# Four-layer gated decoder on one core: keys and values of attention layers 3 and 4 projected ahead of their loops

## The chip, the cores and the metric

The kernel runs on one core of one Trainium2 chip. The metric is the device time of one execution in microseconds (us). The kernel uses all engines of the core: PE (TensorE), DVE (VectorE), ACT (ScalarE), POOL (GpSimd) and SP, which issues transfers.

## The reference

A decoder with four stages. Each adds a gated cross-attention and a gated feed-forward network (FFN) to `x` of 64 sequences x 64 tokens x 128 features. `ctx` has the same shape and doesn't change. The sizes written in the helper functions of the reference are not those of the inputs: attention has 16 heads of 8 features and 64 keys per sequence.

```python
x = x + tanh(g_xattn[0]) * L0_attention(q=norm(x), k=ctx, v=ctx)
x = x + tanh(g_ffn[0])   * L0_ffn(norm(x))                      # int8 SwiGLU
x = x + tanh(g_xattn[1]) * L1_attention(k=ctx, q=norm(x), v=ctx, mask)   # causal
x = x + tanh(g_ffn[1])   * L1_moe(norm(x))                      # 8 experts, top 2
x = x + tanh(g_xattn[2]) * L2_attention(q=norm(x), k=ctx, v=ctx)
x = x + tanh(g_ffn[2])   * L2_ffn(norm(x))                      # block-quantised
x = x + tanh(g_xattn[3]) * L3_attention(query=norm(x), key=ctx, value=ctx)
x = x + tanh(g_ffn[3])   * L3_ffn(norm(x))                      # 4-bit quantised
```

Each attention projects queries from the normalised `x`, and keys and values from `ctx` by weights of its own; then come scores, softmax over the 64 keys, the weighted values and an output projection. Keys and values of every layer hang on `ctx` alone.

## The kernel before

Every engine has a program of its own, written out by hand, and they meet at semaphores. The order of the work is the order of the lines; no scheduler moves anything. The 4096 tokens are 32 tiles of 128 (two sequences each), in `x_sb` all through; `ctxT` holds the context turned, features on partitions. Two buffers (s or x = 0, 1) alternate between tiles.

**An attention layer** (`attention(l)`, l = 0 to 3, once on each engine) is a software pipeline. `attention_order` calls `half` for t = -3 to T + 2, with the tiles that each step works on: `new` = t for scores, `ahead` = t + 1 for its key and query, `later` = t + 2 for its normalised rows, `prev` = t - 1, `old` = t - 2 and `oldest` = t - 3 for what comes behind the softmax. In layers 1 and 3 the steps with t < 0 are done elsewhere. In one step PE does, in this order: the scores of tile t (L674, 16 small matmuls); the transposes of `xn` (L640) and of `o_sb` (L649); the key of tile t + 1 (L653) and its query (L655); the values of tile t (L692); the outputs of tile t - 1 (L706, 32 small matmuls); the output projection of t - 2 (L720), in layer 2 with a bias by L722; and the eight transposes of `sm` (L747), the softmax's argument, which end in `ps`. ACT takes the exponential (L1038), copies `oT` and `xnT` out of PSUM (L1052, L1054), writes the values into `vbd` (L975, a block-diagonal operand), the query into `qbd` (L938) and the key into `kT`, twice with different scales (L940; the trace calls the two buffers `q_r` and `q_m`). DVE takes the row maximum (`rowmax`, L1879), subtracts it (`sm`, L1885, two halves), inverts the softmax's denominator (L1825), adds the residual (L1547) and scales the output (L1836). POOL normalises rows (`xn`, L1320). The key of one tile passes like this:

```python
# PE, key_and_query, L651 on
nc.tensor.matmul(project[:, 0:P], wk[l][:, :], ctxT[:, (t + 1) * P:(t + 2) * P], start=True, stop=True)
# ACT, key_and_query, L936 on
last = nc.scalar.activation(kT[y][:, a, :], src[:, 0:P], ACT.Identity, scale=odd_pair[:, a:a + 1], bias=bkp[l][:, a:a + 1])
```

**Layer 2** does more in the same loop: for each tile POOL issues two indirect transfers that gather the experts' rows (L1202), and DVE mixes them into `x_sb` (L1579), until the tiles run out some six steps before the end.

**The routing drain** lies between layer 1 and the experts. Steps T + 3 to T + 9 turn (L543), score (L555) and count (L566 to L571) the last routed tiles. POOL scatters rows to the experts' slots (L1218). When the last tile is chosen, ACT takes the exponential of the gates (L1100); DVE then adds to every tile of `x_sb` the rows that no expert took (L1937, 32 steps), and increments what the experts wait for (L1993). PE runs 26 matmuls whose result nobody reads (`keep_clock`, L509), and then the experts (L768 on).

**The barrier** lies behind the experts. The gathers wait until every expert's output is stored. PE turns the quantised weights of the last FFNs (L812, 20 transposes; ACT copies them, L1124), runs `keep_clock(8)` and enters layer 2, where steps -2, -1 and 0 have a `keep_clock(5)` each.

Of the kernel before, what the change touches and what calls it, by code (L numbers as in the profile page):

```python
# [14 lines left out]
P = 128  # L15
# [25 lines left out]
FP4_WEIGHT_STEPS, MEASURE_STEPS, ROUND_STEPS = 16, 7, 3  # L41
BATCHES = ((0, 8), (8, 16), (16, 22), (22, 27), (27, 32))
# [9 lines left out]
def flamingo(nc, x_d, ctx_d, mask_d, gx_d, gf_d, attn_d, f0_d, moe_d, f2_d, f3_d, const_d, out_d):  # L52
# [28 lines left out]
    def bias_layer(t, since):  # L81


        l, odd = divmod(t - since - 12, 2)
        return l if not odd and 1 <= l < 4 else None

# [78 lines left out]
    with ExitStack() as stack:  # L165
# [132 lines left out]

        def variances(s, i, n):
            return mv_all[:, :].rearrange("p (i s c) -> p s c i", s=NS, c=2)[:, s, 1, i - n + 1:i + 1]  # L300
# [34 lines left out]
        attn_in, small_in, w0_in, blk_in, mask_in = (sem(n) for n in ("attn_in", "small_in", "w0_in", "blk_in", "mask_in"))  # L335
# [5 lines left out]
        ZERO_SET, VBD_SET, ONES_SET, RSTD_FIRST, RAW_TURNED, WMAX_SHARED = 1, NS + 1, 3 * NS + 1, 3 * NS + 2, 3 * NS + 3, 3 * NS + 4  # L341
# [5 lines left out]
        v_psum, v_taken = sems("v_psum"), sems("v_taken")  # L347
        bst_ready = sems("bst_ready")
# [20 lines left out]
        out_done, scatters_late = sem("out_done"), sem("scatters_late")  # L369
# [5 lines left out]
        def _(sp):  # L375
# [44 lines left out]
            for a in range(2):  # L420
                sp.dma_start(amask_u8[a * S:(a + 1) * S, :].rearrange("q (b k) -> q b k", k=S), mask_d.rearrange("b q k -> q b k")).then_inc(mask_in, 16)
# [62 lines left out]
        def _(pe):  # L484
# [20 lines left out]
            def keep_clock(n, out=bank(1, 2)):  # L505


                for _ in range(n):
                    nc.tensor.matmul(out, ones_b[:, :], amask[:, 0:512], start=True, stop=True, skip_group_check=True)  # L509
# [109 lines left out]
            def attention(l):  # L619
                k = ATTENTION_STAGE[l]  # L620

                def half(t, x, fetch, further, later, ahead, new, prev, old, oldest):
# [64 lines left out]
                    if new is not None:  # L687
                        for b in range(2):
                            for a in range(2):
                                cols = wv[l][:, :].rearrange("d (r a w) -> d a r w", a=2, w=2 * HD)[:, a, :, :]  # L690
                                dst = turned[1][a * S:(a + 1) * S, b * S:(b + 1) * S].rearrange("p (r w) -> p r w", r=RG)
# [1392 lines left out]
```

## Time and profile before

| | |
|---|---|
| three runs, us | 1084.51, 1085.5, 1087.7 (median 1085.5) |
| span of the profiled execution, us | 1084.4 |
| PE busy | 898.7 us, 83% |
| PE weight loads busy | 707.4 us, 65% |
| DVE busy | 885.9 us, 82% |
| ACT busy | 686.2 us, 63% |
| POOL busy | 523.1 us, 48% |

The profiled execution's own time is its span. Busy shares are means over the whole kernel. Where each stage lies, by the trace: layer 1 with the routing ends at about 384 us, the drain lasts to 437, the experts to 531, the barrier to 553, attention 2 to 705, its FFN to 794, attention 3 to 926, and the last FFN to the end. A row of the timeline gives the start, the duration, the engine, the line and the names; in brackets stands how long the engine was idle before it and what ended that. Matmuls of the same line that follow each other are merged in one row. A row of the groups by line gives the names and shapes, the count, the busy time in us, the mean of one in ns, and the idle time in us in front of them with what ended it. A row of a stretch gives its limits and length, busy us (and count) of PE, PE's weight loads, DVE, ACT and POOL, the granted clock of PE as a share of its full 2.4 GHz (0.50 is 1.2 GHz), the share of the DMA engines and GB/s.

### The profile page before, as it was taken

To read this page: it belongs to the slowest core of one execution; us is meant where nothing else is said; L and a number is where in the kernel's file an instruction comes from. 1 tells how busy PE (TensorE), PEld (TensorE's weight loads), DVE (VectorE), ACT (ScalarE), POOL (GpSimd) and SP (SyncE) were. 2 spreads that over 40 slices of the span, in tenths; PEclk is the share of its full clock that TensorE was granted. 3 is DMA by queue.
4 is the path that set the end of the run, shared out by engine and by line. 5 is a ranking of instruction groups with operands and counts; after the bars stand their busy time and mean duration, and the time that the engine had idled before them with its cause. 6 is when DMAs were issued, how large, how long until landed. Compare 5 with 4: busy or idle time off the path is not lost.

```text
span 1084.4 us, 30129 instructions
## 1 busy us (share of the span) xinstructions
PE 898.7 (83%) x11539; PEld 707.4 (65%) x11557; DVE 885.9 (82%) x2296; ACT 686.2 (63%) x1794; POOL 523.1 (48%) x612
## 2 busy tenths in 40 slices
PE   8999999999999932999689999978899999434443
PEld 5888889978887721566457778834478888222222
DVE  6999888878999961567568889889978888899997
ACT  6888864377776610444447777866678888555553
POOL 6444412254367676223287787255553332355554
PEclk9999999999999966899889999988899999655665
DMA  8760000000000012365111111000000000000000
GB/s 214 186 241 2 3 2 2 1 2 3 3 24 27 27 46 76 114 187 175 51 33 32 26 31 29 6 1 2 1 2 2 2 3 3 1 10 16 15 15 24
DMA packets 60526, 44.42 MB, mean 41 GB/s; under 512 B 15196, under 2 KB 55781, under 8 KB 59366
## 3 DMA queue, kind: packets, MB, share of 16 engines
q1 hardware_dynamic: 55718, 34.09, 10.6%
q0 software_dynamic: 4096, 8.34, 2.7%
q8 instruction: 90, 1.47, 0.6%
q14 instruction: 46, 0.38, 0.1%
q10 hardware_dynamic: 576, 0.13, 0.1%
HBM read 23.73 MB, written 18.87 MB: 39 GB/s over the span
## 4 chain that ended last, share of the span: by engine, by line
PE 63%; DVE 21%; issue 6%; POOL 5%; ACT 2%; DVEq 2%; DMA 1%; POOLq 0%; another core or an unknown queue 0%; SPq 0%; ACTq 0%
PE ps L747 10%; PE ps L706 9%; PE ps L674 7%; PE ps L586 4%; PE ps L720 4%; PE ps L692 4%; POOL q_out L1232 3%; DVE rowmax L1879 3%; PE ps L782 3%; PE ps L791 3%; PE ps L783 3%; PE ps L640 2%; PE ps L655 2%; PE ps L653 2%; DVE sm L1885 2%
## 5 line engine op out<-in xcount | busy, mean ns | idle before, releaser
L1879 DVE TENSOR_REDUCE rowmax<-ps 128x16 f32<-128x1024 f32 x128 | 155.8, 1217 | 35.7 <-PE ps L674 34.4
L1885 DVE TENSOR_TENSOR sm<-ps,rowmax 128x512 f32<-128x512 f32 x256 | 164.9, 686 | 3.4
L1038 ACT ACTIVATE pr<-ps 128x512 f32<-128x512 f32 x256 | 138.9, 595 | 38.2 <-PE ps L747 36.0
L747 PE MATMUL ps<-cst,sm 128*128 128x128 f32 x1024 | 138.9, 277 | 13.3 <-DVE sm L1885 12.2
L706 PE MATMUL ps<-vbd,pr 128*64 128x18 f32 x4096 | 140.3, 211 | 0.5 <-ACT pr L1038 0.5
L706 PEld LDWEIGHTS ps<-vbd,pr 128*64 128x64 f32 x4096 | 134.2, 138 | 1.4 <-ACT pr L1038 1.3
L1320 POOL TENSOR_SCALAR xn<-x_sb,mv_all,rstd_all 128x128 f32<-128x128 f32 x122 | 98.2, 805 | 71.7 <-PE ps L640 65.7
L747 PEld LDWEIGHTS ps<-cst,sm 128*128 128x128 f32 x1024 | 112.8, 141 | 26.3 <-issue 19.5
L938 ACT ACTIVATE qbd<-ps,bqp,cst 128x128 f32<-128x128 f32 x256 | 104.6, 463 | 6.2 <-PE ps L655 2.4
L975 ACT ACTIVATE vbd<-ps 64x128 f32<-64x128 f32 x256 | 70.8, 277 | 34.2 <-PE ps L692 26.6
L1202 POOL DMA_INDIRECT big<-expert_out,row_g x64 | 68.2, 1066 | 49.9 <-DMA expert_out<-xn_all 22.8
L1218 POOL DMA_INDIRECT slots<-xn_all,row_s x64 | 65.0, 1015 | 35.8 <-DVE sm L1885 16.9
L1232 POOL TENSOR_TENSOR big<-big 128x640 f32<-128x640 f32 (+2 forms) x36 | 39.0, 1105 | 82.8 <-DVE big L1761 62.8
L606 PE MATMUL ps<-ident_b,q_out 128*128 128x128 bf16 x64 | 11.5, 277 | 78.8 <-POOL q_out L1232 78.6
L1194 POOL TENSOR_TENSOR rstd_all<-mv_all,cst 128x1 f32<-128x1 f32 x64 | 36.1, 567 | 78.2 <-DVE mv_all L1864 37.8
L1052 ACT ACTIVATE oT<-ps 128x128 f32<-128x128 f32 x128 | 35.5, 277 | 49.1 <-PE ps L649 47.3
L606 PEld LDWEIGHTS ps<-ident_b,q_out 128*128 128x128 bf16 x64 | 4.2, 106 | 92.6 <-POOL q_out L1232 89.0
L1208 POOL TENSOR_TENSOR rstd_all<-mv_all,cst 128x1 f32<-128x1 f32 x60 | 34.5, 575 | 61.3 <-DVE mv_all L1858 50.3
L720 PE MATMUL ps<-wo,oT 128*128 128x128 f32 x256 | 61.0, 320 | 1.2 <-ACT oT L1052 1.2
L1232 POOL TENSOR_TENSOR q_out<-q_r,q_s 128x1280 bf16<-128x1280 f32 (+2 forms) x18 | 37.9, 2104 | 47.7 <-DVE q_r L1692 45.1
L1547 DVE SCALAR_TENSOR_TENSOR x_sb<-ps,tg,x_sb 128x128 f32<-128x128 f32 x192 | 55.0, 290 | 5.2 <-PE ps L857 2.9
L692 PE MATMUL ps<-wv,ctxT 128*64 128x64 f32 x1024 | 58.1, 235 | 0.1
(299 smaller groups left out, 2348.3 us busy)
## 6 DMA issues: line engine op xcount, KB each, us to landing
slots<-hT SPq DMA_DIRECT2D x8, 1024.0 KB, 11.0
sm<-slots SPq DMA_DIRECT2D x32, 256.0 KB, 3.3
expert_out<-xn_all SPq DMA_DIRECT2D x16, 256.0 KB, 3.0
ew<-in_L_ffn_w SPq DMA_DIRECT2D x24, 128.0 KB, 2.6
out<-x_sb SPq DMA_DIRECT2D x32, 64.0 KB, 1.5
slots<-xn_all,row_s POOLq DMA_INDIRECT x64
big<-expert_out,row_g POOLq DMA_INDIRECT x64
x_sb<-in_x SPq DMA_DIRECT2D x1, 512.0 KB, 4.6
```

The costliest lines, as they stand in the source:

```text
L674: last = nc.tensor.matmul(bank(0, r)[:, b * P:(b + 1) * P], qbd[x][rows, b * S:(b + 1) * S, :].rearrange("d q h -> d (q h)"), kT[x][rows, ...
L692: last = nc.tensor.matmul(dst, ctxT[:, t * P + b * S:t * P + (b + 1) * S], cols, start=True, stop=True, skip_group_check=True)
L706: last = nc.tensor.matmul(dst[:, :, h2, :], probs[:, h2, :], heads[:, :, h2, :], start=True, stop=True, skip_group_check=True)
L720: last = nc.tensor.matmul(mixed[:, M_Y], oT[x][:, :], wo[l][:, :], start=True, stop=(l != 2))
L747: last = nc.tensor.transpose(turned[b][:, r * P:(r + 1) * P], sm[x][:, c:c + P], ident)
L938: nc.scalar.activation(qbd[y][:, :, a], src[:, P:2 * P], ACT.Identity, scale=parity[:, a:a + 1], bias=bqp[l][:, a:a + 1])
L975: last = nc.scalar.activation(dst, src[part, :].rearrange("p (r h w) -> p r h w", h=2, w=HD), ACT.Copy)
L1038: nc.scalar.activation(pr[y][:, b, :], turned[b], ACT.Exp, scale=SCALE).then_inc(p_ready[y], 1)
L1232: return nc.gpsimd.tensor_tensor(dst.rearrange("p (n w) -> p n w", w=width), src.rearrange("p (n w) -> p n w", w=width), factor.unsqueeze( ...
L1320: nc.gpsimd.tensor_scalar(xn[buf][:, :], xt, mv_all[:, 2 * u:2 * u + 1], rstd_all[:, u:u + 1], ALU.subtract, ALU.mult).then_inc(xn_ready[b ...
L1879: v.tensor_reduce(row3, sc, AX.X, ALU.max).then_inc(rowmax_ready[x], 1)
L1885: v.tensor_tensor(sm[x][:, :].rearrange("p (r g k) -> p r g k", r=RG, k=S)[:, part], sc[:, part], row3[:, part].unsqueeze(3).broadcast_to( ...
```

## The change

The keys and values of layers 2 and 3 (`KEPT`) are no longer projected inside the layers' loops. They are projected in groups of four tiles: a key group is one matmul with 512 columns, a value group 16 matmuls with 64, each into a PSUM bank of its own out of four (two groups in flight). ACT copies each group to SBUF unscaled, 16 copies per layer, into buffers that are idle there (`big`, `gate`, `ew`, `amask`, `xn_all`) and one new one (`v_late`). In the loops ACT builds `kT` and `vbd` from SBUF. Layer 2's eight groups are projected in the routing drain. Of layer 3's, five come after the weight transposes in the barrier, and three in steps -3, -2 and -1 of layer 2. PE waits for all copies of layer 2 before the experts, and for all of layer 3 at t = 0 of layer 2. `keep_clock(8)` in the barrier and `keep_clock(5)` in steps -2 and -1 of layer 2 go; the idle matmuls now read `cst`, since `amask` is overwritten. The filling of `vbd` waits for the outputs of two tiles before (`o_psum`), not for values in PSUM. Two semaphores are merged into others, which changes no order. The diff, cut:

```diff
+GROUP, GROUPS, KEPT = 4, T // 4, (2, 3)
...
+    def kept_number(l, g):
+        return GROUPS * (l - 2) + (g if l == 2 else (g - GROUPS // 2) % GROUPS)
...
+        kept_keys = {
+            2: [big[:, c:c + GW] for c in (1024, 1536, 2048, 2560, 7168, 7680)] + gate,
+            3: [big[:, 3328 + g * GW:3328 + (g + 1) * GW] for g in range(GROUPS - 1)] + [ew[0][:, 0:2, :].rearrange("p n d -> p (n d)")]}
+        kept_values = {
+            2: [a[:, g * GW:(g + 1) * GW] for a in (amask[:, :].bitcast(F32), v_late) for g in range(GROUPS // 2)],
+            3: [xn_all[:, g * GW:(g + 1) * GW] for g in range(GROUPS)]}
...
+            def value_products(l, t, dst):
+                for b in range(2):
+                    for a in range(2):
+                        cols = wv[l][:, :].rearrange("d (r a w) -> d a r w", a=2, w=2 * HD)[:, a, :, :]
+                        last = nc.tensor.matmul(dst[a * S:(a + 1) * S, b * S:(b + 1) * S].rearrange("p (r w) -> p r w", r=RG),
+                                                ctxT[:, t * P + b * S:t * P + (b + 1) * S], cols, start=True, stop=True, skip_group_check=True)
+                return last
+            def keys_ahead(l, g):
+                n = kept_number(l, g)
+                if n >= 2:
+                    pe.wait_ge(ahead_kept, 2 * n - 3)
+                nc.tensor.matmul(bank(0, 2 * (n % 2)), wk[l][:, :], ctxT[:, g * GW:(g + 1) * GW], start=True, stop=True, skip_group_check=True
+                                 ).then_inc(ahead_psum, 1)
+            def values_ahead(l, g):
+                n = kept_number(l, g)
+                if n >= 2:
+                    pe.wait_ge(ahead_kept, 2 * n - 2)
+                for t in range(GROUP):
+                    last = value_products(l, g * GROUP + t, bank(0, 1 + 2 * (n % 2))[:, t * P:(t + 1) * P])
+                last.then_inc(ahead_psum, 1)
...
                         if ahead is not None:
-                            nc.tensor.matmul(project[:, 0:P], wk[l][:, :], ctxT[:, (t + 1) * P:(t + 2) * P], start=True, stop=True)
+                            if l not in KEPT:
+                                nc.tensor.matmul(project[:, 0:P], wk[l][:, :], ctxT[:, (t + 1) * P:(t + 2) * P], start=True, stop=True)
...
+                    if l == 2 and t == 0:
+                        pe.wait_ge(ahead_kept, 4 * GROUPS)
...
-                    if l == 2 and -2 <= t <= 0 or l == 3 and t == 0:
+                    if l == 2 and t < 0:
+                        keys_ahead(3, t + 4)
+                        values_ahead(3, t + 4)
+                    if l in KEPT and t == 0:
                         keep_clock(5, mixed)
...
             for t in range(T + 3, T + 10):
                 turn_routed(t, 1 - t % NS)
+                if t > T + 3:
+                    keys_ahead(2, t - T - 4)
                 reuse_routing_bank(t, t % NS)
                 score_routed(t, 1 - t % NS)
                 count_batch(t)
+                if t > T + 3:
+                    values_ahead(2, t - T - 4)
+            for g in range(GROUPS - 2, GROUPS):
+                keys_ahead(2, g)
+                values_ahead(2, g)
...
             keep_clock(26)
+            pe.wait_ge(ahead_kept, 2 * GROUPS)
...
+            for g in (4, 5, 6, 7, 0):
+                keys_ahead(3, g)
+                values_ahead(3, g)
             pe.wait_ge(wt_ready, 5)
             pe.wait_ge(early_eps[0], EARLY + 1)
-            keep_clock(8)
...
+            def keep_keys(l, g):
+                n = kept_number(l, g)
+                act.wait_ge(ahead_psum, 2 * n + 1)
+                nc.scalar.activation(kept_keys[l][g], bank(0, 2 * (n % 2)), ACT.Copy).then_inc(ahead_kept, 1)
...
-                    last = nc.scalar.activation(kT[y][:, a, :], src[:, 0:P], ACT.Identity, scale=odd_pair[:, a:a + 1], bias=bkp[l][:, a:a + 1])
+                    last = nc.scalar.activation(kT[y][:, a, :], keys, ACT.Identity, scale=odd_pair[:, a:a + 1], bias=bkp[l][:, a:a + 1])
...
+                    if new is not None and l in KEPT:
+                        act.wait_ge(o_psum[x], IT * l + new)
+                        values(x, tile_of(kept_values[l], t))
...
             for t in range(T + 3, T + 10):
                 empty_routed(t, 1 - t % NS)
+                if t > T + 3:
+                    keep_keys(2, t - T - 4)
+                    keep_values(2, t - T - 4)
+            for g in range(GROUPS - 2, GROUPS):
+                keep_keys(2, g)
+                keep_values(2, g)
             act.wait_ge(e_ready, 1)
             nc.scalar.activation(ge[:, 0, :], ge[:, 1, :], ACT.Exp).then_inc(e_ready, 1)
```

How the instructions stand on PE in the last steps of the drain, before (`xrT` is a routed tile turned, `oh` its choices, `hid` an expert's rows):

```order
L543 MATMUL ps<-cst,xn_all 128x128
L555 MATMUL ps<-rw,xrT 128x8
L566 MATMUL ps<-oh,tri_b 128x80
L568 MATMUL ps<-carry,ones_b 128x80
L571 MATMUL ps<-oh,ones_b 128x2x32
L571 MATMUL ps<-oh,ones_b 128x2x24
L571 MATMUL ps<-oh,ones_b 128x2x16
L571 MATMUL ps<-oh,ones_b 128x2x8
L509 MATMUL ps<-amask,ones_b 128x512 x26
L773 MATMUL ps<-cst,hid 128x128 x8
```

And after the change (L544 is a key group, L536 a value group; the last turn of a routed tile stands in the first row):

```order
L587 MATMUL ps<-cst,xn_all 128x128
L544 MATMUL ps<-ctxT,wk 128x512
L599 MATMUL ps<-rw,xrT 128x8
L536 MATMUL ps<-wv,ctxT 64x64 x16
L544 MATMUL ps<-ctxT,wk 128x512
L536 MATMUL ps<-wv,ctxT 64x64 x16
L544 MATMUL ps<-ctxT,wk 128x512
L610 MATMUL ps<-oh,tri_b 128x80
L612 MATMUL ps<-carry,ones_b 128x80
L615 MATMUL ps<-oh,ones_b 128x2x32
```

Two groups and a key now stand in front of the last count, and five groups and a value group between it and the 26 idle matmuls. On ACT, with their waits, before:

```order
L930 ACTIVATE xrT<-ps 128x128 [waits rT_psum1]
L1100 ACTIVATE ge<-ge 128x32 [waits e_ready]
L934 ACT_TABLE_LOAD
```

and after, the last of the sixteen copies:

```order
L994 ACTIVATE gate_both<-ps 128x512 [waits ahead_psum]
L1003 ACTIVATE v_late<-ps 128x512 [waits ahead_psum]
L1182 ACTIVATE ge<-ge 128x32 [waits e_ready]
L989 ACT_TABLE_LOAD
```

The exponential of the gates stands behind all copies. PE in the barrier, from the weight transposes to the first scores, before:

```order
L812 MATMUL ps<-ident_b,big 128x128 x20
L509 MATMUL ps<-amask,ones_b 128x512 x8
L640 MATMUL ps<-cst,xn 128x128
L509 MATMUL ps<-amask,ones_b 128x512 x5
L653 MATMUL ps<-ctxT,wk 128x128
L655 MATMUL ps<-xnT,wq 128x128
L640 MATMUL ps<-cst,xn 128x128
L509 MATMUL ps<-amask,ones_b 128x512 x5
L674 MATMUL ps<-q_r,qbd 128x128 x8
```

and after, from the last of six groups on:

```order
L544 MATMUL ps<-ctxT,wk 128x512
L536 MATMUL ps<-wv,ctxT 64x64 x16
L684 MATMUL ps<-cst,xn 128x128
L544 MATMUL ps<-ctxT,wk 128x512
L536 MATMUL ps<-wv,ctxT 64x64 x16
L700 MATMUL ps<-xnT,wq 128x128
L684 MATMUL ps<-cst,xn 128x128
L544 MATMUL ps<-ctxT,wk 128x512
L536 MATMUL ps<-wv,ctxT 64x64 x16
L721 MATMUL ps<-q_r,qbd 128x128 x8
```

Six groups stand in front of the first turn of `xn` (L640, now L684), and two more between it and the first scores (L674, now L721).

## Rows read from the trace of the kernel before

**Rows 1.** Groups by line, DVE, mixing part of attention 2 (573.5 to 680.5 us)

```profile
L1825 DVE RECIPROCAL rden<-ps 128x16 f32<-128x16 f32 x22 | 5.7, 258 | 11.5 <-PE ps L722 9.0 <-remote 2.3
```

**Rows 2.** Timeline of one tile of attention 3

```profile
851.48 0.54 PEld L674 LDWEIGHTS ps<-q_r,qbd 32*128 32x128 f32 x16 [0.22 <-ACT q_r L940]
852.27 1.22 DVE L1879 TENSOR_REDUCE rowmax<-ps 128x16 f32<-128x1024 f32 x1 [0.57 <-PE ps L674]
...
852.30 0.30 PEld L653 LDWEIGHTS ps<-ctxT,wk 128*128 128x128 f32 x2
...
852.95 0.31 PEld L692 LDWEIGHTS ps<-wv,ctxT 128*64 128x64 f32 x8
...
853.45 0.56 ACT L975 ACTIVATE vbd<-ps 64x128 f32<-64x128 f32 x2 [0.33 <-PE ps L692]
...
856.39 1.23 DVE L1879 TENSOR_REDUCE rowmax<-ps 128x16 f32<-128x1024 f32 x1 [0.56 <-PE ps L674]
```

**Rows 3.** Timeline, first tiles of attention 3

```profile
798.83 1.22 DVE L1879 TENSOR_REDUCE rowmax<-ps 128x16 f32<-128x1024 f32 x1 [1.44 <-PE ps L674]
...
800.92 1.16 PE L747 MATMUL ps<-cst,sm 128*128 128x128 f32 x8 [0.16 <-DVE sm L1885]
...
802.84 1.23 DVE L1879 TENSOR_REDUCE rowmax<-ps 128x16 f32<-128x1024 f32 x1 [0.97 <-PE ps L674]
```

**Rows 4.** Groups by line and shape, ACT, whole span

```profile
L940 ACT ACTIVATE q_r<-ps,bkp,odd_pair 128x128 f32<-128x128 f32 x128 | 51.4, 459 | 0.0
...
L949 ACT ACTIVATE hT<-x_sb,mean_in,rstd_all 128x128 f32<-128x128 f32 x32 | 14.0, 497 | 0.0
```

**Rows 5.** Timeline of two tiles in the mixing part of attention 2

```profile
579.97 1.00 POOL L1202 DMA_INDIRECT big<-expert_out,row_g  x1 [0.30 <-issue]
...
580.07 0.39 PE L722 MATMUL ps<-y_bias_b,cst 128*128 128x128 f32 x2
...
581.57 0.26 DVE L1825 RECIPROCAL rden<-ps 128x16 f32<-128x16 f32 x1 [0.90 <-PE ps L722]
...
603.89 0.39 PE L722 MATMUL ps<-y_bias_b,cst 128*128 128x128 f32 x2
...
604.31 1.01 POOL L1202 DMA_INDIRECT big<-expert_out,row_g  x1 [0.30 <-issue]
...
605.84 0.26 DVE L1825 RECIPROCAL rden<-ps 128x16 f32<-128x16 f32 x1 [0.79 <-remote]
```

**Rows 6.** Timeline, row maxima of the last tiles of attention 2

```profile
688.93 1.22 DVE L1879 TENSOR_REDUCE rowmax<-ps 128x16 f32<-128x1024 f32 x1 [0.48 <-PE ps L674]
...
701.70 1.23 DVE L1879 TENSOR_REDUCE rowmax<-ps 128x16 f32<-128x1024 f32 x1 [0.51 <-PE ps L674]
```

**Rows 7.** Timeline of the routing drain and the first expert

```profile
399.66 0.23 ACT L1100 ACTIVATE ge<-ge 128x32 f32<-128x32 f32 x1 [6.96 <-issue]
...
402.88 1.38 DVE L1937 SCALAR_TENSOR_TENSOR x_sb<-xn_all,wx,x_sb  x4 [0.18 <-issue]
...
430.25 7.88 DVE L1937 SCALAR_TENSOR_TENSOR x_sb<-xn_all,wx,x_sb  x20 [5.25 <-issue]
...
437.64 2.05 PE L782 MATMUL ps<-q_r,ew 128*128 128x512 f32 x2 [1.65 <-DVEq L1993]
...
443.83 1.02 PE L782 MATMUL ps<-q_r,ew 128*128 128x512 f32 x2
```

**Rows 8.** Busy time and granted clock of two stretches, drain and barrier

```profile
392.00:394.00 2.00, 0.96 (x4) 0.60 (x3) 1.03 (x8) 0.28 (x1) 1.69 (x2) 0.50 0.20 66
540.00:542.00 2.00, 0.93 (x3) 0.51 (x5) 0.96 (x5) 0.00 (x0) 1.55 (x2) 0.50 0.27 66
```

**Rows 9.** Timeline of the barrier behind the experts

```profile
534.01 0.38 PE L812 MATMUL ps<-ident_b,big 128*128 128x128 bf16 x4 [0.29 <-ACT wT L1124]
...
549.55 0.73 PE L674 MATMUL ps<-q_r,qbd 32*128 32x128 f32 x16
...
553.50 1.19 DVE L1879 TENSOR_REDUCE rowmax<-ps 128x16 f32<-128x1024 f32 x1
```

More of the change, by code:

```diff
@@ L85, in bias_layer, with tile_of @@
         return l if not odd and 1 <= l < 4 else None
+    def kept_number(l, g):
+        return GROUPS * (l - 2) + (g if l == 2 else (g - GROUPS // 2) % GROUPS)
+    def tile_of(groups, t):
+        return groups[t // GROUP][:, t % GROUP * P:(t % GROUP + 1) * P]
     def turned_context(t):
@@ L508, in keep_clock @@
                 for _ in range(n):
-                    nc.tensor.matmul(out, ones_b[:, :], amask[:, 0:512], start=True, stop=True, skip_group_check=True)
+                    nc.tensor.matmul(out, ones_b[:, :], cst[:, 0:256].bitcast(BF16), start=True, stop=True, skip_group_check=True)
+            def value_products(l, t, dst):
[18 more added lines that the diff above has]
+                last.then_inc(ahead_psum, 1)
             def turn_context(t):
@@ L686, in half @@
                         pe.wait_ge(p_ready[y], 2 * (IT * l + prev) + 2)
[L687 to L691, printed above, removed]
-                                last = nc.tensor.matmul(dst, ctxT[:, t * P + b * S:t * P + (b + 1) * S], cols, start=True, stop=True, skip_group_check=True)
-                        last.then_inc(v_psum[x], 1)
+                    if new is not None and l not in KEPT:
+                        value_products(l, t, turned[1][:, 0:P]).then_inc(v_psum[x], 1)
                     if oldest is not None:
@@ L847, in ffn2 @@
                     pe.wait_ge(hid_ready[0], IT)
-                    nc.tensor.matmul(bank(0, 1)[:, 0:P], wk[3][:, :], ctxT[:, 0:P], start=True, stop=True)
                 if px is not None:
@@ L934, in load_table, with keep_values, key_and_query @@
                 nc.scalar.activation(g_sb[:, 0:1], tg[:, 0:1], func)
-            def key_and_query(l, y, src):
+            def keep_keys(l, g):
+                n = kept_number(l, g)
+                act.wait_ge(ahead_psum, 2 * n + 1)
+                nc.scalar.activation(kept_keys[l][g], bank(0, 2 * (n % 2)), ACT.Copy).then_inc(ahead_kept, 1)
+            def keep_values(l, g):
+                n = kept_number(l, g)
+                if (l, g) == (3, 0):
+                    for p in range(2):
+                        for s in range(NS):
+                            act.wait_ge(eo_stored[p][s], 16 * E // 2)
+                act.wait_ge(ahead_psum, 2 * n + 2)
+                nc.scalar.activation(kept_values[l][g], bank(0, 1 + 2 * (n % 2)), ACT.Copy).then_inc(ahead_kept, 1)
+            def key_and_query(l, y, src, t):
+                keys = tile_of(kept_keys[l], t) if l in KEPT else src[:, 0:P]
                 for a in range(2):
@@ L1063, in half @@
                         project_ahead()
+                    if l == 2 and t < 0:
+                        keep_keys(3, t + 4)
+                        keep_values(3, t + 4)
                     if l == 0 and t == T:
@@ L1125, in _ @@
             load_table(ACT.Exp)
+            for g in (4, 5, 6, 7, 0):
+                keep_keys(3, g)
+                keep_values(3, g)
+            act.wait_ge(ahead_kept, 2 * GROUPS)
             attention(2)
+            act.wait_ge(ahead_kept, 4 * GROUPS)
             def ffn2(c, x, h, px, ph):
```

30 lines of the change are left out of this document (17 added, 13 removed).

## The prediction

> **What bounds the kernel now.** The change touches four places: the routing drain (about 384 to 437 us), the barrier behind the experts (531 to 553), and the third and fourth attention layers, called attention 2 and attention 3 as in the code (553 to 705 and 794 to 926). I went to each in turn. The first view to read is the list of groups by line, for DVE, in the part of attention 2 where the experts' rows are gathered and mixed in [rows 1]: 22 tiles take 107 us, 4.86 each, and what DVE waited for was the softmax's denominator, 11.5 us in front of the reciprocal. Whether PE or the gathers stand behind that wait decides what the change can give here; it is taken up below.
>
> Attention 3 has no gathers. In order of time [rows 2], rowmax starts at 852.27 and again at 856.39, a period of 4.12 us. Between them PE has 0.30 us of weight loads for the key projection and 0.31 for the values; ACT waits 0.33 for the values before it can fill vbd; and DVE waits 0.57 for scores. Two tiles at the start of the layer show the floor that lies under this [rows 3]: there PE reached the transposes of sm early and waited 0.16 us for DVE, and the rowmaxes still stand 4.01 us apart (798.83 to 802.84), with DVE waiting for scores before each. That loop is rowmax, sm, the last four transposes, the next tile's scores, rowmax; no key or value projection is in it.
>
> **Attention 3.** Removed per tile: one key matmul and four value matmuls, about 0.5 us of PE (0.30 and 0.31 less their overlap with neighbours) [rows 2]. That is not the gain. PE now arrives early, and sm is what it waits for: the period falls from 4.12 to the 4.01 of the floor, which gives 0.11. With some 28 tiles in that state the term is **-3.1 us**. ACT could be late next, since kT and vbd now come from SBUF. The nearest rows are L949, which reads SBUF, at 497 ns, and L940, which reads PSUM, at 459 [rows 4]: 38 ns more on each of four instructions is 0.15, against the 0.33 wait that goes. So ACT gains 0.18 where 0.11 is needed, and stays just off the path. Bounds: 0 (ACT takes over the loop) and -0.5 a tile, -15 (all the removed PE time is gained, which the floor excludes).
>
> **Attention 2.** In the mixing part nothing is gained, by this reading [rows 5]. The reciprocal at 581.57 waited 0.90 us, and the profile names PE's L722, which had ended at 580.46. If that were the cause the lag would be constant. It is 1.11 there, and 1.56 at 605.84, where L722 ended by 604.28. Measured from the end of POOL's gather (580.97, 605.32) the two lags are 0.60 and 0.52. So I hold that POOL releases DVE, not PE. Term 0; bounds -8 (rival A) and +5 (the gathers fall less well between DVE's steps). The last four tiles have no gathers and run like attention 3. Three of their periods take 12.77 us, 688.93 to 701.70 [rows 6], 4.26 each; down to the floor of 4.01 that is 0.25, four times: **-1.0**, between 0 and that.
>
> **The routing drain.** Added to PE from about 392, where its last matmuls on routed tiles stand [rows 8]: eight groups of one 512-column key matmul and sixteen value matmuls. A pair with 512 columns takes 1.02 us at 443.83, at full clock, and 2.05 at 437.64, at half [rows 7]; a tile of values 0.31 [rows 2]. So a group is 1.02 + 4 x 0.31 = 2.3 us, or 4.5 at half. PE is at half clock here, 0.50 over 392 to 394 [rows 8], and the experts' first matmuls took 6.2 us (437.64 to 443.83) to leave it. 6.2 us at half hold 1.4 groups, 6.6 more take 15: PE is done at about 413.5. Three things stand behind it. The batch count waits for two and a half groups; the scatters that need its rows are queued behind others that POOL issues without a pause, so I cost that at nothing (some 10 us of cover). The 26 clock matmuls start later, nothing. But the exponential of the gates, 399.66 now, stands behind all sixteen copies on ACT, so it moves to about 414, and DVE's loop that adds the routed rows (32 steps) with it. Twelve of its 32 steps were done by 430.25; the other 20 then took 7.88 us, and PE's first expert matmul waited 1.65 us for the end of that loop [rows 7]. With 16 us instead of 30 ahead of 430.25, half of the twelve are done, and six more at 0.39 come behind: **+2.4**. Bounds: +4.7 (none of the twelve done) and -1.65 (the loop is done in time). Why the later ones of the twelve were so slow the trace does not say: four of the first six took 1.38 us together, at 402.88, and scatters ran beside those as well [rows 7]. So I take the slowness as something the first half escaped, and the term as it stands. A rule of the Trainium skill reads it otherwise. "GPSIMD Engine Reference", key points, has GpSimd sharing its SBUF interfaces with VectorE, with contention for DVE instructions that have two SBUF inputs, as this one has. By it no step beside the scatters would be quick, so a loop that starts at 414 does hardly any of the twelve, and the term goes to its upper bound, +4.7; the quick steps at 402.88 speak against it.
>
> **The barrier.** PE's last weight transpose ends at 534.39, and tile 0's scores were at 549.55 [rows 9]. Removed are 18 clock matmuls; added, in front of the first transpose of xn, six groups, 13.8 us: to 548. Two more stand in front of the scores, which must also wait for ACT's last copies: 553 plus 1 is 554. The scores themselves can be late, since rowmax started only at 553.50, 3.2 us after their end, behind DVE's mixing; scores at 554 give a rowmax at about 554.8 (0.79 behind them, as at 851.48 and 852.27) [rows 2]: **+1.3**. This takes the full clock, as the dense work behind 437.64 came to it. Bounds: 0, and +12 (six groups at half clock, 27 us).
>
> **Sum.** -3.1 - 1.0 + 2.4 + 1.3 = -0.4 us. The profiled execution spans 1084.4, 0.1% under the median of the three runs, 1085.5; I take the difference off the median: **1085.1 us**.
>
> **Rivals.** *A, PE does pay in attention 2.* The profile names L722 for 9.0 of the 11.5 us in front of the reciprocal [rows 1], and with 0.5 us less work L722 comes 0.5 earlier. If that freed DVE, about 0.3 of each of some 25 tiles would go: -7.5, so 1077.6. Against it are the two lags. Chance 0.20. *B, slower: the block in the barrier runs at half clock.* PE has been thinly busy before it, and the clock was 0.50 over 540 to 542, where the clock matmuls start [rows 8]. If it falls under the added block, six groups take 27 us instead of 14, and the first rowmax comes some 12 us late. The sum is then +10: 1096; half of that, a clock that comes back inside the block, 1090. The change is slower than before once this place costs more than 1.7 us, and measurably so from 5.0. For it: that half clock. Against it: dense work brings the clock back within 6.2 us [rows 7]. Chance 0.17. *C, attention 3 pays nothing*, because ACT's SBUF reads take what its wait gave, and the periods stay: +3.7 (1089) for all of it, or +2.7 (1088) with the tail of attention 2 gained. For it, only 0.07 us a tile separates ACT from the path; against, the wait of 0.33 does go. Chance 0.13. My forecast has 0.50.
>
> **How the numbers follow.** A measurement of this kernel tells a change from none at about 0.3%, 3.3 us: 1082.2 and 1088.8 are the limits. The forecast's own range is 1081 to 1088.5 (the drain from -1.65 to +4.7, the barrier up to +2.5), a fifth of it under 1082.2: faster 0.10, same 0.38, slower 0.02. A gives faster 0.20. B gives slower 0.16, same 0.01. C gives same 0.07, slower 0.06. Together: faster 0.30, same 0.46, slower 0.24. The range of 8 in 10 takes in A, C and the milder half of B: 1077 to 1090.
>
> **What would show it.** Right, if in attention 3 the rowmaxes stand 3.95 to 4.05 apart and PE waits for sm before most transposes; if the mixing part of attention 2 keeps about 4.86 a tile; if the exponential comes at 410 to 416 and the first expert matmul 1 to 4 us later than 437.64; and if the first rowmax of attention 2 comes 1 to 3 us later counted from the experts' end. Wrong, if the period in attention 3 is 4.1 with ACT in front of the scores (C), or under 3.9 (then the floor was misread); if tiles of attention 2 fall under 4.6 (A); or if the clock is half over 534 to 550 (B).

## The result, and the profile after

The changed kernel takes **1104.3 us** (median of 4 runs, 1100.4 to 1108.4), against 1085.5 before: a ratio of **1.017**, interval 1.0149 to 1.0192. It is slower by some 19 us, where I forecast no change, and outside my range (1077 to 1090). Measured again the ratio was 1.0181 (1.0157 to 1.0206). The profiled execution spans 1101.3 us, 16.9 more than the one of before.

Where they come from, by the distance between landmarks that both traces have (us). The first expert matmul is L782 (now L835), the last weight transpose L812 (now L866), rowmax L1879 (now L1966).

| stretch | before | after | difference | forecast |
|---|---|---|---|---|
| start to last rowmax of attention 1 | 377.99 | 378.98 | +1.0 | 0 |
| drain: to the first expert matmul | 59.65 | 79.49 | **+19.8** | +2.4 |
| experts: to the last weight transpose | 96.37 | 96.61 | +0.2 | 0 |
| barrier: to the first rowmax of attention 2 | 19.49 | 23.45 | **+4.0** | +1.3 |
| attention 2, first to last rowmax | 148.20 | 142.74 | **-5.5** | -1.0 |
| to the first rowmax of attention 3 | 93.14 | 94.24 | +1.1 | 0 |
| attention 3, first to last rowmax | 127.34 | 123.58 | **-3.8** | -3.1 |
| to the end | 162.22 | 162.21 | 0.0 | 0 |

The loops gained what they could, and more than I gave them. The drain took it back twice. The list of waits of the changed kernel, over the drain (384 to 460 us; line waited for, us in total, times, longest), says how:

```profile
PEld ps L536 <- issue: 27.4, 28, 2.5
DVE gk L2008 <- ACT ge L1182: 22.0, 1, 22.0
ACT amask L1003 <- remote: 21.6, 2, 18.5
DVE pre L1691 <- PE ps L615: 21.5, 1, 21.5
...
PE ps L536 <- issue: 19.1, 27, 1.7
...
POOL slots L1305 <- DVE row_s L1734: 8.7, 1, 8.7
```

PE stood still 19.1 us inside the value matmuls (L536), and what ended these gaps is "issue": no semaphore, no engine. In the code none of these matmuls but a group's first waits for anything. (The label alone would not show that; in the second experiment it also stands in front of waits for a semaphore.) The timeline of PE shows the shape:

```profile
396.70 1.12 PE L544 MATMUL ps<-ctxT,wk 128*128 128x512 f32 x2
397.76 0.50 PE L536 MATMUL ps<-wv,ctxT 128*64 128x64 f32 x9
398.67 0.26 PE L536 MATMUL ps<-wv,ctxT 128*64 128x64 f32 x1 [0.41 <-issue]
400.08 0.30 PE L536 MATMUL ps<-wv,ctxT 128*64 128x64 f32 x2 [1.15 <-issue]
401.52 0.26 PE L536 MATMUL ps<-wv,ctxT 128*64 128x64 f32 x1 [1.15 <-issue]
...
417.05 0.34 PE L536 MATMUL ps<-wv,ctxT 128*64 128x64 f32 x1 [0.46 <-issue]
417.31 2.08 PE L544 MATMUL ps<-ctxT,wk 128*128 128x512 f32 x2
419.18 0.27 PE L610 MATMUL ps<-oh,tri_b 128*128 128x80 bf16 x1
...
443.48 5.79 PE L530 MATMUL ps<-cst,ones_b 128*128 128x512 bf16 x26
...
458.47 2.05 PE L835 MATMUL ps<-q_r,ew 128*128 128x512 f32 x2 [8.33 <-DVEq L2080]
```

The first group and part of the second run at the pace I took for them. From 398.3 on, one to three matmuls come through every 0.7, 1.4 or 2.1 us. A single one is still short (0.22 to 0.37 us); what is missing is the next one. The last count (L610) stands behind it, at 419.18; it was at 396.33 before, so it comes 22 us later, counted from the end of attention 1. ACT was late as well: its copy of the first value group, whose matmuls had ended at 396.8, started at 414.22, though ACT had been free since 395.7 (timeline, ACT):

```profile
414.22 0.60 ACT L1003 ACTIVATE amask<-ps 128x512 f32<-128x512 f32 x1 [18.48 <-remote]
```

POOL's timeline has the other half:

```profile
413.36 0.97 POOL L1305 DMA_INDIRECT slots<-xn_all,row_s  x1 [0.30 <-issue]
422.98 0.97 POOL L1305 DMA_INDIRECT slots<-xn_all,row_s  x1 [8.65 <-DVE row_s L1734]
...
434.47 0.97 POOL L1305 DMA_INDIRECT slots<-xn_all,row_s  x1 [0.30 <-issue]
```

POOL's scatters ran one behind the other up to 414.3. PE picked up its pace 3 us later. POOL then had nothing to scatter, since the rows of the last tiles hang on the late count; from 422.98 to 435.4 it scattered the rest, and PE stalled again from 427.2 to 437.2. The cover that I gave the count was there, and larger than my 10 us: before, the rows stood ready at 399.5 and the first of these ten scatters was issued at 413.8. But the count came 22 us late, and the last scatter ended 9 us later than before (435.4 against 426.3). What comes behind all copies came last (timeline, ACT and DVE):

```profile
444.08 0.22 ACT L1182 ACTIVATE ge<-ge 128x32 f32<-128x32 f32 x1
...
446.48 0.63 DVE L2024 SCALAR_TENSOR_TENSOR x_sb<-xn_all,wx,x_sb  x2 [0.35 <-DVE wx L2014]
447.29 11.83 DVE L2024 SCALAR_TENSOR_TENSOR x_sb<-xn_all,wx,x_sb  x30 [0.18 <-issue]
```

The exponential moved from 399.66 [rows 7] to 444.08. DVE's 32 steps lie whole between it and the experts; with the scatters over, they take 12.6 us with hardly a gap.

In attention 3 the floor was read right. These rows answer to those of before [rows 2, 3]:

```profile
867.30 1.22 DVE L1966 TENSOR_REDUCE rowmax<-ps 128x16 f32<-128x1024 f32 x1 [0.48 <-PE ps L721]
...
868.03 0.63 ACT L1045 ACTIVATE vbd<-xn_all 64x128 f32<-64x128 f32 x2
...
870.49 0.54 PEld L721 LDWEIGHTS ps<-q_r,qbd 32*128 32x128 f32 x16 [0.17 <-ACT q_r L1010]
871.28 1.23 DVE L1966 TENSOR_REDUCE rowmax<-ps 128x16 f32<-128x1024 f32 x1 [0.48 <-PE ps L721]
```

The period is 3.98 us, and `vbd` waits for nobody. What SBUF costs ACT is in the groups by shape:

```profile
L1010 ACT ACTIVATE q_r<-ps,bkp,odd_pair 128x128 f32<-128x128 f32 x64 | 25.7, 459 | 0.0
...
L1010 ACT ACTIVATE q_r<-big,bkp,odd_pair 128x128 f32<-128x128 f32 x52 | 22.7, 487 | 0.0
...
L1045 ACT ACTIVATE vbd<-xn_all 64x128 f32<-64x128 f32 x64 | 19.8, 309 | 0.4
```

28 ns more for a key copy and 32 for a value copy (277 before): 0.12 us a tile, where I had 0.15.

### The profile page after: what moved, and what is told of

Read it like the earlier page. It is cut to its first block, busy times and chain, and to the rows that moved or that the text cites. A ratio compares the mean times of both kernels' runs of the same rounds, so it can differ in the third digit from the quotient of the medians.

```text
span 1101.3 us, 29957 instructions
## 1 busy us (share of the span) xinstructions
PE 920.1 (84%) x11443; PEld 701.8 (64%) x11443; DVE 882.6 (80%) x2296; ACT 707.4 (64%) x1826; POOL 522.3 (47%) x612
## 4 chain that ended last, share of the span: by engine, by line
PE 65%; DVE 21%; issue 6%; POOL 3%; ACT 2%; DVEq 1%; DMA 0%; SPq 0%; POOLq 0%; another core or an unknown queue 0%; ACTq 0%
PE ps L793 10%; PE ps L748 9%; PE ps L721 6%; PE ps L536 4%; PE ps L630 4%; PE ps L762 4%; DVE rowmax L1966 3%; PE ps L835 3%; POOL q_out L1319 3%; PE ps L844 3%; PE ps L836 3%; PE ps L684 2%; DVE sm L1972 2%; PE ps L700 2%; PE ps L640 2%
## 5 line engine op out<-in xcount | busy, mean ns | idle before, releaser
L1966 DVE TENSOR_REDUCE rowmax<-ps 128x16 f32<-128x1024 f32 x128 | 155.8, 1217 | 35.6 <-PE ps L721 34.2
L793 PE MATMUL ps<-cst,sm 128*128 128x128 f32 x1024 | 143.6, 279 | 23.4 <-DVE sm L1972 20.1
L748 PE MATMUL ps<-vbd,pr 128*64 128x18 f32 x4096 | 143.1, 213 | 0.7 <-ACT pr L1108 0.5
L793 PEld LDWEIGHTS ps<-cst,sm 128*128 128x128 f32 x1024 | 110.3, 141 | 46.5 <-issue 34.7
L536 PE MATMUL ps<-wv,ctxT 128*64 128x64 f32 x1024 | 58.3, 239 | 21.6 <-issue 21.5
L536 PEld LDWEIGHTS ps<-wv,ctxT 128*64 128x64 f32 x1024 | 42.4, 144 | 44.6 <-issue 32.9
```

Source lines behind the costliest of these rows:

```text
L536: last = nc.tensor.matmul(dst[a * S:(a + 1) * S, b * S:(b + 1) * S].rearrange("p (r w) -> p r w", r=RG), ctxT[:, t * P + b * S:t * P + (b ...
L748: last = nc.tensor.matmul(dst[:, :, h2, :], probs[:, h2, :], heads[:, :, h2, :], start=True, stop=True, skip_group_check=True)
L793: last = nc.tensor.transpose(turned[b][:, r * P:(r + 1) * P], sm[x][:, c:c + P], ident)
L1966: v.tensor_reduce(row3, sc, AX.X, ALU.max).then_inc(rowmax_ready[x], 1)
```

## The experiments

**Is it the order on ACT alone?** In this kernel the exponential stands in front of the copies of groups 2 to 7:

```diff
             for t in range(T + 3, T + 10):
                 empty_routed(t, 1 - t % NS)
                 if t > T + 3:
                     keep_keys(2, t - T - 4)
                     keep_values(2, t - T - 4)
+                if t == T + 5:
+                    act.wait_ge(e_ready, 1)
+                    nc.scalar.activation(ge[:, 0, :], ge[:, 1, :], ACT.Exp).then_inc(e_ready, 1)
...
-            act.wait_ge(e_ready, 1)
-            nc.scalar.activation(ge[:, 0, :], ge[:, 1, :], ACT.Exp).then_inc(e_ready, 1)
```

> The changed kernel with one thing moved: on ACT the exponential of the gates stands in front of the copies of groups 2 to 7, not behind all sixteen. Starvation (PE gets its instructions too slowly while POOL's scatters run one behind the other, so the added stretch of small matmuls stalls, and the count behind it comes late): PE's gaps named issue stay (about 19 us in the drain), the exponential comes a few us behind the late count, at about 423 us, PE is through its groups at about 443 as now, and the first expert matmul moves from 458.5 to 446 to 452; in all 1091 to 1098 us. Order on ACT alone (the step of the prediction): the exponential comes at 400 to 404, the first expert matmul at 438 to 441, in all 1084 to 1088.

Measured: 1103.6 us, ratio 1.0155 (1.0126 to 1.0183). PE's gaps are there again (21.2 us named issue), the exponential comes at 421.26 and the first expert matmul at 451.44, 6 us nearer to attention 1 than in the changed kernel. So the place on ACT accounts for 6 of the 20 us, and PE's stall stands with either order: DVE's loop is over at 444.2, and the experts wait for PE itself, which is through its groups at 444.6. The total I expected (1091 to 1098) was missed. The drain's 6 us and 2.9 in the experts were given back, 3.2 in the barrier (26.64 us), 4.5 in attention 2 (147.28) and 2.1 behind it; these lengths differ between kernels with the same loop, as below.

**Is it the number of small instructions?**

```diff
-                for t in range(GROUP):
+                if l == 2:
+                    last = nc.tensor.matmul(bank(0, 1 + 2 * (n % 2)), wv[l][:, :], ctxT[:, g * GW:(g + 1) * GW], ...)
+                for t in range(GROUP if l == 3 else 0):
                     last = value_products(l, g * GROUP + t, bank(0, 1 + 2 * (n % 2))[:, t * P:(t + 1) * P])
```

> The changed kernel in which each value group of layer 2 is one matmul with 512 columns instead of sixteen with 64: about the same PE time (1.0 us against 1.2 at full clock), 4 instructions instead of 64; the values of attention 2 are not the reference's. The order on ACT stays. Starvation by the number of instructions: no gaps named issue over 1 us, PE through the groups by 412 to 418, the exponential at 412 to 418, first expert matmul at 438 to 444, in all 1083 to 1090 us. Contention for SBUF or PSUM, or the half clock, as the cause: the same data stream is read and written, so the groups stay slow, PE ends near 440 and the time stays over 1098.

Measured: 1096.3 us, ratio 1.0092 (1.0062 to 1.0122): a miss for both. Five groups go through without a gap named issue, and the last count is in time, at 398.4. But from 400 on ACT's copies are late, and PE with them (timeline of both engines):

```profile
401.81 1.02 PE L544 MATMUL ps<-ctxT,wk 128*128 128x512 f32 x2
...
404.83 0.60 ACT L996 ACTIVATE big<-ps 128x512 f32<-128x512 f32 x1 [2.24 <-PE ps L552]
...
405.48 1.12 PE L544 MATMUL ps<-ctxT,wk 128*128 128x512 f32 x2 [1.72 <-issue]
409.06 0.60 ACT L1005 ACTIVATE amask<-ps 128x512 f32<-128x512 f32 x1 [3.63 <-remote]
...
409.71 2.07 PE L552 MATMUL ps<-ctxT,wv 128*128 128x512 f32 x2 [3.10 <-issue]
412.62 0.60 ACT L996 ACTIVATE big<-ps 128x512 f32<-128x512 f32 x1 [2.96 <-PE ps L552]
...
413.27 2.07 PE L544 MATMUL ps<-ctxT,wk 128*128 128x512 f32 x2 [1.49 <-issue]
```

ACT copies the groups in their order, keys before values. The copy at 412.62 is that of the fifth key group, whose matmul (401.81) had ended at 402.8, and ACT's copy before it was over at 409.66: ACT itself was 3 us late, and it executes a handful of instructions here. PE was not: a group may start only when the copy of two groups before has emptied its bank, and each of these gaps ends 0.05 us behind such a copy (405.43, 409.66, 413.22), whatever the label says. So on PE the stall went with the sixteen small matmuls. ACT is late without any long stream, and the exponential, behind all copies, came at 432.07.

**Is it the scatters?** Both kernels without 26 of the 28 scatters of the drain (their rows don't reach the experts, which compute with what the buffer held):

```diff
-                    for c in range(2):
+                    for c in range(2 if u == T - 1 else 0):
                         scatter(b, u, c)
...
-            sp.wait_ge(sent, 16 * 2 * T)
+            sp.wait_ge(sent, 16 * 2 * (T - 13))
```

> The changed kernel without 26 of the 28 scatters that POOL issues in the routing drain (tiles 18 to 30; those rows don't reach the experts); the two of tile 31 stay, so the experts still wait for the last choice. If the scatters are what starves the engines: the gaps named issue in the drain are gone, PE's eight groups are through by 412 to 416 (starting at about 392, 1.4 groups at half clock, the rest at full), the exponential comes by 417, DVE's 32 steps take 12.6 us without a gap, first expert matmul at 430 to 433. If the count of small instructions alone does it (an instruction stream that PE cannot be fed at this pace anywhere): the gaps stay with about 19 us, and PE ends near 440.

> The kernel before without the same 26 scatters. If the scatters starve every engine and not PE alone: DVE's loop over 32 tiles, which stood idle for some 24 us between its first 12 steps before, runs through in 12.6 us from 402 on, and ends at 415. If its slowness is its own (its branch, its registers): it keeps steps 2 to 5 us apart and ends near 438.

Measured, the changed kernel: the eight groups run from 392.3 to 411.0, somewhat earlier than I expected, with no gap of PE inside a group,

```profile
396.90 1.15 PE L536 MATMUL ps<-wv,ctxT 128*64 128x64 f32 x32
397.99 1.12 PE L544 MATMUL ps<-ctxT,wk 128*128 128x512 f32 x2
398.95 0.20 PE L610 MATMUL ps<-oh,tri_b 128*128 128x80 bf16 x1
...
409.89 1.15 PE L536 MATMUL ps<-wv,ctxT 128*64 128x64 f32 x32
411.20 5.56 PE L530 MATMUL ps<-cst,ones_b 128*128 128x512 bf16 x25 [0.16 <-issue]
```

the exponential at 411.58, and the first expert matmul at 427.42. The kernel before: DVE's loop over the tiles, with 24.4 us of gaps named issue in the original (one of them is the 5.25 before 430.25 [rows 7]), runs through. Its line in the list of waits of the original, and its rows without scatters:

```profile
DVE x_sb L1937 <- issue: 24.4, 9, 5.2
...
403.98 0.63 DVE L1937 SCALAR_TENSOR_TENSOR x_sb<-xn_all,wx,x_sb  x2 [0.35 <-DVE wx L1927]
404.79 11.37 DVE L1937 SCALAR_TENSOR_TENSOR x_sb<-xn_all,wx,x_sb  x30 [0.18 <-issue]
```

That settles what the gaps hang on. Without the scatters the same instructions run at pace, on PE and ACT in one kernel and on DVE in the other. The edit takes away POOL's issuing and the transfers together, so it doesn't say which of the two it is. (The times of the two, 1083.3 and, from a single run, 1068.6 us, also leave out the scatters' own 26 x 1.28 us, and are no measure of a useful kernel. Nor is the drain: it is 49.32 against 35.97 us, 13.4 apart. With no scatters to wait for, the delay of the exponential (33.5 us behind attention 1 against 21.4) is paid in full. What such a delay costs beside scatters is in the kernels below that keep the keys alone.)

**Which layer, and which part, is worth keeping?** Layer 3 alone, keys and values:

```diff
-GROUP, GROUPS, KEPT = 4, T // 4, (2, 3)
+GROUP, GROUPS, KEPT = 4, T // 4, (3,)
```

(with the drain's calls taken out and the counts adapted)

> Only layer 3 (attention 3) is projected ahead; attention 2 projects in its loop as before, nothing is added to the routing drain, the barrier keeps its five groups and the three in steps -3 to -1. Starvation in the drain as the main loss: the drain is as before (first expert at 437 to 439), attention 3 keeps its 3.98 us a tile (-3.8), the barrier costs up to 4, in all 1083 to 1088 us; attention 2 goes back to about 4.8 a tile. Rival (the loss has its seat in the barrier or in SBUF reads of the loops): over 1095.

Measured: 1091.1 us, ratio 1.0042 (1.0027 to 1.0057). The drain is as before (59.63), attention 3 at 3.98 a tile, attention 2 back at 148.83; but the barrier costs 6.5 us (26.01). The total is 3 us over what I expected, and the barrier is why. Its groups meet POOL's gathers. In the changed kernel PE stands still 2.4 us among the value matmuls there (timeline, PE):

```profile
561.34 0.62 PE L536 MATMUL ps<-wv,ctxT 128*64 128x64 f32 x9
562.37 0.22 PE L536 MATMUL ps<-wv,ctxT 128*64 128x64 f32 x1 [0.41 <-issue]
563.08 0.33 PE L536 MATMUL ps<-wv,ctxT 128*64 128x64 f32 x3 [0.50 <-issue]
564.52 0.81 PE L536 MATMUL ps<-wv,ctxT 128*64 128x64 f32 x19 [1.11 <-issue]
```

With layer 3 alone it is 1.5 us, the granted clock is 0.54 to 0.61 over the first group (533 to 537), and the scores of tile 0 wait 2.8 us for ACT's last copy (list of waits, 533 to 559 us):

```profile
PE ps L721 <- ACT xn_all L995: 2.8, 1, 2.8
...
PE ps L536 <- issue: 1.5, 2, 1.1
```

Then the keys alone, of both layers, with the values in the loops, the idle matmuls restored, and the exponential in front of the copies of groups 2 to 7 as in the first experiment:

```diff
-                    if new is not None and l not in KEPT:
+                    if new is not None:
                         value_products(l, t, turned[1][:, 0:P]).then_inc(v_psum[x], 1)
...
             for g in (4, 5, 6, 7, 0):
                 keys_ahead(3, g)
-                values_ahead(3, g)
```

> Only the keys of both layers are projected ahead (one matmul of 512 columns a group, 4 instructions); the values stay in the loops; the idle matmuls of the barrier are back; the exponential stands in front of the copies of groups 2 to 7. Starvation: the drain is nearly as before (first expert at 437 to 441). Attention 3: the key matmul is about half of the PE time that the change takes away, and 0.14 us a tile is all that the loop can give, so 3.98 to 4.05 a tile; attention 2 between 4.60 and 4.78; in all 1076 to 1083 us. Rival: it takes the values out too to reach the floor (ACT's wait for the values stays), attention 3 stays at 4.08 to 4.12, in all 1083 to 1088.

Measured: **1082.9 us against 1086.7, ratio 0.9968** (0.9952 to 0.9983), faster than before by 0.3%, and within what I expected. Attention 3 is at 3.98 a tile with the value matmuls still in its loop. The drain is 59.90 us, the barrier 19.55, both as before. Two variants of it:

> Only the keys of layer 3 are projected ahead (five groups in the barrier, three in steps -3 to -1 of attention 2, the idle matmuls there kept); nothing in the drain, attention 2 as before. If attention 2 gains by less work on PE (rival A of the prediction, at least in part): attention 3 gives its 3.9 us, attention 2 takes 148 to 149 us as before against 142.7 to 147.3 with its keys kept, in all 1081 to 1084 us, some 1 to 3 above the kernel with the keys of both layers. If attention 2's length only scatters with the phase of the gathers: the same time as with the keys of both layers, within 1 us.

> The kernel with the keys of both layers, but the exponential of the gates behind all eight copies, as the change has it. PE's key groups end at about 404.5, so by the prediction's own step the exponential comes at about 405 and the loop that adds the routed rows starts some 5 us later; while it is slow it does a step in 2 to 5 us, so one to three steps more are left behind 430, 0.4 us each: first expert matmul at 438 to 439, 0.4 to 1.2 us more in all. If ACT and PE starve here too, as they did with one matmul a value group: exponential after 415, first expert matmul at 440 or later, 2 to 5 us more.

Keys of layer 3 alone (the same edit with KEPT = (3,)): 1082.8 us against 1087.0, ratio **0.9953** (0.9939 to 0.9968), attention 2 at 147.12. So the keys of layer 2 buy nothing that can be told from zero in the total, and the smallest version is as good as any here. With the exponential behind the eight copies: 1083.7, ratio 0.9968 (0.995 to 0.9985); exponential at 410.44, first expert matmul at 439.09, drain 61.03 us, +1.1 against the order with the exponential early. This is the size the step of my prediction had in mind, and it holds where few instructions meet the scatters. ACT was late here too: PE's last key group ended at 405.3, and the last copy started at 409.95.

**Does PE pace attention 2?** The kernel before with the projections of layer 2 issued twice, and with them left out from tile 2 on, but for one value matmul (stale PSUM is read; the output isn't the reference's):

```diff
-                            nc.tensor.matmul(project[:, 0:P], wk[l][:, :], ctxT[:, ...], start=True, stop=True)
+                            for _ in range(2 if l == 2 else 1):
+                                nc.tensor.matmul(project[:, 0:P], wk[l][:, :], ctxT[:, ...], start=True, stop=True)
...
```

(the value matmuls likewise)

> The kernel before, with the key matmul and the four value matmuls of attention 2 issued twice each: 0.5 us more PE work a tile in that layer, nothing else. If PE is on the path of the mixing part (rival A): attention 2 grows by 0.2 to 0.5 us a tile, 5 to 15 us in all. If POOL's gathers pace it and PE has slack (the forecast's reading): the mixing part grows by less than 1.5 us, and only the last four tiles, which have no gathers, by some 0.4 each; in all +1 to +3 us.

> The kernel before, with the key matmul and three of the four value matmuls of attention 2 left out from tile 2 on (PSUM keeps old numbers; the output of the layer is not the reference's): about 0.45 us less PE work a tile in that layer, no projection ahead, no copies, the same reads on ACT. Rival A: attention 2 takes 141 to 145 us instead of 148, in all 3 to 7 us less. The forecast's reading: only the last four tiles gain, attention 2 takes 147 to 148, in all 0 to 1.5 us less.

Measured on one chip, where the kernel before took 1070.4 us: more PE work 1085.0, ratio 1.0128 (1.0111 to 1.0145); less PE work 1070.0, ratio 1.000 (0.999 to 1.001). With more, PE was busy in 126.47 of 127 us, at 4.79 us a tile: there it is PE that paces the loop. With less, attention 2 took 133.23 us, 4.30 a tile, yet the total did not fall. From these totals I take it that on that chip the original loop already ran near 4.3 and had nothing to gain, while the added matmuls cost 14.6 us in all. That chip ran the kernel before 15 us faster than the others, so I measured once more:

> The kernel before, profiled once more, since its median was 1085 to 1087 us beside most kernels and 1070.4 beside the two with more and less PE work in attention 2. If the difference lies in attention 2 (two rhythms of gathers, DVE and PE, one near 4.3 us a tile and one alternating about 4.4 and 5.1): a run near 1070 has attention 2 at 133 to 137 us, a run near 1086 at 147 to 149, and the other stages agree within 1 us. If the chip as a whole differs: every stage is 1 to 2% shorter in the fast case.

> The changed kernel once more, on the same chip as the run above. Starvation by the scatters doesn't hang on the rhythm of attention 2: the drain costs its 19 to 21 us again (first expert matmul 79 to 81 us behind the last row maximum of attention 1, against 59.7), the barrier 4 to 8. Beside a before of 1086: 1100 to 1108 us. Beside a before of 1070, where attention 2 has nothing left to gain: 1092 to 1108, a ratio of 1.02 to 1.035.

The chip was one of the usual kind: 1089.3 and 1106.4 us beside a before of 1086.9. Attention 2 took 148.16 and 142.73 us, the drain 59.83 and 80.69, the barrier 19.54 and 25.46. The change's losses repeat. Why one chip runs the kernel before in 1070 us stays open, as no trace of that kernel was taken there; so what PE's work is worth in attention 2 isn't settled either.

## Why the prediction was wrong

**The routing drain: the step that failed.** "6.2 us at half hold 1.4 groups, 6.6 more take 15: PE is done at about 413.5" priced each matmul by its duration and its clock, and took for granted that PE, and ACT behind it, is handed its next instruction in time. Without scatters PE was done at 411.0: the sum of durations was right, 2.5 us on the high side. With them PE was done at 443.5. The same blindness is in "the scatters that need its rows are queued behind others that POOL issues without a pause, so I cost that at nothing": the cover was real, some 14 us, and the count came 22 us late. The exponential, costed at 14 us of delay, had 44.

**The warning stood in my rows.** DVE's steps beside the scatters were 2 to 5 us apart with "issue" in front of them [rows 7], 24.4 us in all, and I wrote that the trace does not say why. I then put the slowness down as a property of that loop, beside an addition of PE work in the same 30 us. A gap named issue on one engine, in code that waits for nothing there, was the sign that others may starve beside it. The Trainium skill's rule that I weighed ("GPSIMD Engine Reference", key points: shared SBUF interfaces, contention with DVE instructions of two SBUF inputs) is about GpSimd and DVE. If that contention lengthened the DVE instruction, the rows would show it, and they don't: a step takes 0.35 us beside scatters too, and it is the next one that is missing. PE and ACT, of which that rule does not speak, starve as well. The bound that I took from it (+4.7) was as far off as mine.

**The barrier.** +1.3 against +4.0, and 4 to 8.3 in the six profiles that have these groups. In this profile it was not rival B: the clock was 1.00 all over the block (windows of the changed kernel).

```profile
556.00:558.00 2.00, 2.00 (x35) 1.31 (x34) 0.00 (x0) 1.97 (x4) 1.70 (x2) 1.00 0.15 39
...
562.00:564.00 2.00, 0.54 (x4) 0.32 (x4) 1.32 (x5) 0.00 (x0) 1.67 (x3) 1.00 0.14 33
```

It looks like the same starvation, here beside gathers, which no run took away: PE busy 2.00 of 2 us at first, 0.54 of 2 six us later. The price of six groups, 13.8 us, became 16.4 (555.3 to 571.7), and that is the whole miss in this profile. In the other five PE's gaps among value matmuls are shorter (0.7 to 2.3 us against 2.4), but two more things come in: the clock was at or near half for some 4 to 6 us of the block, which is rival B in small, and the scores waited 2.4 to 3.0 us for ACT's last copy.

**Attention 3: right in mechanism, and nearly in size.** The period fell to the floor: 3.98, not 4.01, and over all 31 intervals, -3.8 against -3.1. ACT stayed off the path, with 0.12 us more where I had 0.15. What I had not seen is that the values need not be moved for it: 0.14 us a tile is less than the key matmul alone.

**Attention 2: too little.** The tail gave 0.8 of its 1.0. The part before it gave 4.6 where I had 0. My two lags were no proof: with its projections gone the layer took between 142.7 and 147.3 us in five profiles, and 147.1 to 148.8 in five with them in the loop (144.4 and 148.8 with the keys alone ahead), so the gain lies between nothing and 6 us, by how gathers, DVE and PE fall into step, and rival A holds in part at most. Two kernels with the same loop differed by 4.5 us there.

**The sum.** -3.1 - 1.0 + 2.4 + 1.3 became -3.8 - 5.5 + 19.8 + 4.0, and 2.3 that come and go between profiles of the same kernel (the stretch between the two layers took 93.1 us in one profile of the kernel before and 96.4 in the other).

## What to carry to other kernels

Before moving work into an engine's idle time, look at what the other engines do in that time: if any of them has gaps that end in "issue" with nothing to wait for, work placed there may not run at its durations. Where indirect transfers are issued back to back, place few and large instructions or none, and nothing that a later step on the path waits for in order behind them. And move the smallest part that reaches the floor: here one 512-column matmul per four tiles gave all of attention 3's gain, and the sixteen small ones beside it, with the copies that follow them, cost some twenty microseconds in the drain.

## What the runs showed of the hardware

While POOL issues indirect transfers one behind the other (one each 1.28 us), other engines can get their next instruction late:

- DVE, in the kernel before: 24.4 us of gaps in a loop of 32 steps of 0.35 us.
- PE, in the changed kernel: 19.1 us of gaps among matmuls with 64 columns.
- ACT, among copies: one started 17 us behind its matmuls in the changed kernel, and the copies with one matmul a value group 2 to 5 us behind the moment when they could.

The starts then lie mostly a multiple of 0.70 us apart: 0.7, 1.4 or 2.1 on PE, 2.1 to 5.6 on DVE and ACT. The lateness begins 4 to 14 us after the run of scatters begins and ends some 4 us or less behind its end. It takes scatters: without them the 19.1 and the 24.4 us were gone.

PE isn't always hit. A run of 26 idle matmuls beside the same scatters did not stall in the kernel before (6.8 us for 25, with the clock at 0.50 over 406 to 408 and 1.00 from 410), though DVE starved in the same microseconds. With one 512-column matmul a group, PE's gaps in the drain were waits for ACT's copies.

The instructions themselves are not longer at the same clock. The clock did not start the stall: the granted clock was 0.99 over 396 to 400, where PE's gaps begin. It fell to 0.50 by 404, when PE had stood idle between single matmuls for some us, and a key group behind the stall took 2.08 us (417.31) in place of 1.12 (396.70).

What is short in that time isn't settled. The DMA engines were busy for 15% of 404 to 408. The Trainium skill, "Runtime: NRT & Kernel Launch", section "Instruction fetch mechanics", says that engines fetch instructions ahead in blocks of 256. By that alone one would not expect gaps of 3 us between ACT's few copies; no run here tests it. Spacing the scatters out, or starting them earlier, wasn't tried.
